# Edge loop of a graph-attention layer: two blocks per preparation step, eight row buffers instead of six, first gathers in steps

## What is computed

```python
h = (x @ W).reshape(n, H, C)
a_src = (h * att_src[None]).sum(-1)
a_dst = (h * att_dst[None]).sum(-1)
alpha = a_src[src] + a_dst[dst] + a_edge
alpha = jax.nn.leaky_relu(alpha, NEG_SLOPE)
amax = jax.lax.stop_gradient(jax.ops.segment_max(alpha, dst, num_segments=n))
ex = jnp.exp(alpha - amax[dst])
denom = jax.ops.segment_sum(ex, dst, num_segments=n)
att = ex / (denom[dst] + 1e-16)
msg = h[src] * att[:, :, None]
out = jax.ops.segment_sum(msg, dst, num_segments=n).reshape(n, H * C) + bias
```

## Time and profile before

| what | value |
|---|---|
| median of 3 runs | 3088.73 us (3086.78 to 3095.65) |
| profiled execution, its time | 3089.7 us |
| profiled execution, its span | 3087.9 us |
| the edge loop in it, first gather to last new maximum | 953.97 to 1392.77 us |
| PE, DVE, ACT, POOL busy over the whole span | 81%, 53%, 28%, 19% |
| mean granted TensorE clock | 0.883 |

### The profile page before, as it was taken

The page is one execution under the profiler, slowest core; times in us unless marked ns, Lnnn a source line. Parts: engine busy times, 40 slices in busy tenths (PEclk is TensorE's granted clock), DMA queues, the critical chain, the costliest instruction groups (busy, mean ns, idle before and its releaser), DMA issues. The chain is left out here.

```text
span 3087.9 us, 30949 instructions
## 1 busy us (share of the span) xinstructions
PE 2505.5 (81%) x10585; PEld 1594.7 (52%) x10585; DVE 1646.0 (53%) x3714; ACT 861.9 (28%) x1943; POOL 601.0 (19%) x567
## 2 busy tenths in 40 slices
PE   4877965999955888784578999999998769759886
PEld 1344545999943776672443455444554334534442
DVE  9999344222323888887235897708962432430000
ACT  2165110111112666662111465105631100101110
POOL 0000056355303444431110000000001001012221
PEclk9899966999976888887598999999999889779888
DMA  4000444766734555540533553215434031469996
GB/s 128 0 1 1 139 125 134 255 212 215 248 76 114 141 141 141 146 104 19 192 118 144 188 191 108 76 59 178 162 96 144 0 121 39 175 207 350 342 338 205
DMA packets 198728, 445.53 MB, mean 144 GB/s; under 512 B 26570, under 2 KB 48058, under 8 KB 198094
## 3 DMA queue, kind: packets, MB, share of 16 engines
q1 hardware_dynamic: 156942, 344.67, 33.5%
q0 software_dynamic: 41632, 98.89, 12.3%
HBM read 396.77 MB, written 49.05 MB: 144 GB/s over the span
## 5 line engine op out<-in xcount | busy, mean ns | idle before, releaser
L2166 PE MATMUL psum<-x_res,HH 125*128 125x512 f32 (+1 forms) x960 | 353.4, 527 | 18.2 <-DVE x_res L2356 18.2
L2166 PEld LDWEIGHTS psum<-x_res,HH 125*128 125x128 f32 x960 | 182.0, 193 | 178.9 <-issue 158.1
L1146 POOL DMA_INDIRECT recd<-edge_records,edge_slots x160 | 192.2, 1201 | 328.9 <-issue 322.5
L1506 POOL DMA_INDIRECT hg<-HT,srcidx x196 | 191.5, 977 | 300.8 <-PE psum L1626 172.2
L1667 ACT ACTIVATE hg<-hg,ex 128x129 f32<-128x129 f32 x784 | 235.2, 388 | 1.6
L1626 PE MATMUL psum<-hg,Dh 128*125 128x258 f32 x784 | 231.9, 460 | 4.3 <-DVE ACC L1569 2.9
L2156 PE MATMUL psum<-W,XO 128*125 128x512 f32 x480 | 211.9, 603 | 0.0
L1626 PEld LDWEIGHTS psum<-hg,Dh 128*125 128x125 f32 x784 | 177.1, 232 | 45.1 <-issue 6.2
L2932 PE MATMUL psum<-wd,XN 128*40 128x512 f32 (+1 forms) x704 | 167.7, 635 | 14.6 <-DMA wd<-in_L_ffn_W_down 14.6
L1180 PE MATMUL psum<-xgT,w 128*128 128x192 f32 x1024 | 175.3, 330 | 2.9 <-DMA w<-in_L_ffn_w 2.9
L1180 PEld LDWEIGHTS psum<-xgT,w 128*128 128x128 f32 x1024 | 168.7, 192 | 7.1 <-DMA w<-in_L_ffn_w 4.1
(11 more groups left out here) (508 smaller groups left out, 3942.3 us busy)
## 6 DMA issues: line engine op xcount, KB each, us to landing
wd<-in_L_ffn_W_down SPq DMA_DIRECT2D x30, 2560.0 KB
w<-in_L_ffn_w SPq DMA_DIRECT2D x64, 1024.0 KB, 12.2
MK<-CT SPq DMA_DIRECT2D x80, 625.0 KB
wu<-in_L_ffn_W_up SPq DMA_DIRECT2D x8, 2730.0 KB, 17.7
rows<-ROWS POOLq DMA_DIRECT2D x24, 625.0 KB, 7.5
w<-in_L_ffn_W SPq DMA_DIRECT2D x18, 512.0 KB
t<-in_L_ffn_tv_W SPq DMA_DIRECT2D x16, 512.0 KB
targets<-DROW SPq DMA_DIRECT2D x49, 128.0 KB
```

The source lines that it names most:

```text
L1146: pool.indirect_dma_start(out=g.recd, out_offset=bass.IndirectOffsetOnAxis(ap=g.posi[:, c:c + 1], axis=0), in_=g.E8[:, c, :], in_offset=No ...
L1506: pool.indirect_dma_start(out=hg[j % RING][:, c, :], out_offset=None, in_=g.HT, in_offset=bass.IndirectOffsetOnAxis(ap=g.srcidx[:, j * CH ...
L2166: return pe.matmul(flat[:, at:at + x1 - x0], HH[:, k, h * DH + c * 128:h * DH + c * 128 + 128], z[n % 4][:, x0:x1], start=(k == 0 and i < ...
```

## The change

It rewrites `gnn1_blocks`:

- Blocks go in pairs p = (2p, 2p+1), NP = 25. Slot terms, turn, rows and one-hots are made once per pair at double width. Slot terms of pair p+1 run in the even iteration j = 2p, its one-hots in the odd iteration j = 2p+1. Spread, largest, look-up, alpha, weights, sum and add stay per block.
- `Dh` and `q` have two buffers (of pairs) instead of three (of blocks). SP's loads are 25 of twice the size.
- `hg` is one tensor with eight row buffers. One semaphore counts the gathers of a pair, and the slot terms of a pair wait for all eight of them (L1526 in the changed file).
- Gathers of blocks 0 and 1 are issued at once. Those of blocks 2 to 7 wait for `rows` of pair j // 2 - 1 (`pool.wait_ge(*rows.at(j // 2))`): 2 and 3 for the slot terms of pair 0, and so on. From block 8 on block j waits until block j - 8 is summed.

```diff
-    HW, N4, RING = NH * (DH + 1), CH * NH, 6
+    HW, N4, RING, NP = NH * (DH + 1), 2 * CH * NH, 8, (NB + 1) // 2
...
     def pool_program():
         for j in range(NB):
             if j >= RING:
                 pool.wait_ge(*summed.at(j - RING + 1))
+            elif j >= 2:
+                pool.wait_ge(*rows.at(j // 2))
             for c in range(CH):
...
-    def dve_slot_terms(j):
-        u = j % 3
-        dve.wait_ge(*gathered[j % RING].at(64 * (j // RING + 1)))
-        step(dve.tensor_tensor(q[u][:], hg[j % RING][:, :, HW:HW + NH], rec(j)[:, :, 2:6], ALU.add))
-        if j:
-            dve.wait_ge(*turned.at(j))
+    def dve_slot_terms(p):
+        n, first = chunks(p), 2 * p % RING
+        dve.wait_ge(*gathered[p % (RING // 2)].at(128 * (p // (RING // 2)) + 16 * n))
+        found = hg[:, first:first + n // CH, :, HW:HW + NH].rearrange("p r c h -> p (r c) h")
+        step(dve.tensor_tensor(q[p % 2][:, 0:n, :], found, rec(p)[:, :, 2:6], ALU.add))
+        if p:
+            dve.wait_ge(*turned.at(p))
...
         dve_slot_terms(0)
         dve_onehots(0)
-        dve_slot_terms(1)
         tiles = {}
         for j in range(NB):
             tiles[j] = tile_of(dve, j)
             dve_largest(j)
             dve_new_max(j, tiles[j])
-            if j + 2 < NB:
-                dve_slot_terms(j + 2)
+            if j % 2 == 0 and j // 2 + 1 < NP:
+                dve_slot_terms(j // 2 + 1)
             if j >= 2:
                 dve_add_sums(j - 2, tiles[j - 2])
             dve_alpha(j)
-            if j + 1 < NB:
-                dve_onehots(j + 1)
+            if j % 2 == 1 and j // 2 + 1 < NP:
+                dve_onehots(j // 2 + 1)
...
             pe_look_up(j)
             if j + 1 < NB:
                 pe_spread(j + 1)
-            if j + 2 < NB:
-                pe_turn(j + 2)
+            if j % 2 == 0 and j // 2 + 1 < NP:
+                pe_turn(j // 2 + 1)
             if j:
                 pe_sum(j - 1)
...
             act_rescale(j)
-            if j + 2 < NB:
-                act_rows(j + 2)
+            if j % 2 == 0 and j // 2 + 1 < NP:
+                act_rows(j // 2 + 1)
             act_weights(j)
```

More of the change, by code:

```diff
@@ L1473, in gnn1_blocks @@
     v, selected = s.sig("dve_steps"), s.sig("selector_made")
-    gathered = [s.sig(f"gathered{u}") for u in range(RING)]
+    gathered = [s.sig(f"gathered{u}") for u in range(RING // 2)]
     loaded = [s.sig(f"counts_loaded{u}") for u in range(3)]
@@ L1484, in bank, with chunks, rec, half @@
         return g.PS[0:TP, k, :]
-    def rec(j):
-        return g.rec[:, j * CH:(j + 1) * CH, :]
+    def chunks(p):
+        return min(2, NB - 2 * p) * CH
+    def rec(p):
+        return g.rec[:, 2 * p * CH:2 * p * CH + chunks(p), :]
+    def half(j):
+        return j // 2 % 2, j % 2 * CH
     def tile_of(eng, j):
@@ L1495, in sp_program @@
     def sp_program():
-        for j in range(NB):
-            if j >= 3:
-                sp.wait_ge(*onehot.at(3 * (j - 2)))
-            sp.dma_start(drow[j % 3][:], bcast(g.DROW[j * BLK:(j + 1) * BLK], 128)).then_inc(*loaded[j % 3].up(16))
+        for p in range(NP):
+            if p >= 3:
+                sp.wait_ge(*onehot.at(3 * (p - 2)))
+            n = chunks(p) * 128
+            sp.dma_start(drow[p % 3][:, 0:n], bcast(g.DROW[2 * p * BLK:2 * p * BLK + n], 128)
+                         ).then_inc(*loaded[p % 3].up(16))
     def pool_program():
@@ new lines, in dve_slot_terms @@
+    def dve_slot_terms(p):
[5 more added lines that the diff above has]
+            dve.wait_ge(*turned.at(p))
+        split(dve, step, q[p % 2][:, 0:n, :].rearrange("p c h -> p (c h)"),
+              [q_parts[:, k, 0:n * NH] for k in range(3)], q_rest[:, 0:n * NH]).then_inc(*rows.up())
@@ L1600, in pe_spread @@
     def pe_spread(j):
-        pe.wait_ge(*rowsT.at(j + 1))
+        b, c0 = half(j)
+        pe.wait_ge(*rowsT.at(j // 2 + 1))
         if j:
@@ L1610, in pe_look_up @@
     def pe_look_up(j):
-        b = tile_of(pe, j)
+        tile, (b, c0) = tile_of(pe, j), half(j)
         pe.wait_ge(*newmax.at(j + 1))
@@ L1644, in pe_program, with act_rows @@
         pe_sum(NB - 1)
-    def act_rows(j):
-        act.wait_ge(*turned.at(j + 1))
-        if j >= 2:
-            act.wait_ge(*spread.at(j - 1))
-        act.activation(qT[j % 2][:], g.PS[0:3 * N4, 4, 0:128], ACT.Copy).then_inc(*rowsT.up())
+    def act_rows(p):
+        act.wait_ge(*turned.at(p + 1))
+        if p >= 2:
+            act.wait_ge(*spread.at(2 * (p - 1)))
+        act.activation(qT[p % 2][:], g.PS[0:3 * N4, 4, 0:128], ACT.Copy).then_inc(*rowsT.up())
     def act_rescale(j):
```

71 lines of the change are left out of this document (36 added, 35 removed).

## The result

The changed kernel took 3086.32 us (median; 3081.11 to 3089.94), beside 3091.4 us (3085.17 to 3096.29) for the kernel before on the same chip. The ratio is 0.9984, with an interval from 0.9976 to 0.9992: faster by 0.16%, 5.1 us. The profiled execution has a span of 3083.1 us, 4.8 less than before, at nearly the same granted clock (0.884, before 0.883).

What follows compares the result with a forecast made beforehand. While gathers run, matmul signals held behind POOL's bursts were taken to bound the loop, 8.38 us per block against 8.57 measured. Mid-loop 0, tail -3 and start +3 summed to 0: 3089 us, range 3068 to 3107.

Steps and rivals of the forecast that it cites:

- What bounds the loop: Mid-loop: signals held behind POOL's gathers make a two-block chain, 8.38 us per block; DVE's own chain is 7.72.
- The forecast drawn from it there: From the no-contention rule: gathers have no part in the late signals, DVE's time sets the pace, about 3071 us.
- Price of both edits while gathers run: 0. The cover is the held signal: Mid-loop: cheaper slot terms and one-hots save DVE 0.6 us per block, but the held signal hides it: 0.
- mid-loop 0: The middle of the loop while gathers run: the change was to gain or lose nothing there, 0 us.
- The rival of rarer breaks: Mid-loop: masks only in odd iterations break the hold less often, up to +8 us, 3097; chance 0.10.
- DVE's time counts: Mid-loop: 20 blocks without waits gain 0.6 us each, -12; with tail -3 and start -4, 3071 us; chance 0.32.
- Buffers. ... at the same place of the iteration: Mid-loop gathers still follow a sum, four at a time; eight buffers help only the loop's end, tail -3 us.
- With the cover gone: Mid-loop: were the held signal gone, DVE's shorter work would save 41 x 0.6 = 25 us.
- The start, +3: First gathers: -4 us from earlier data, +6 for three bursts of eight, +1 for loads; ends -4 and +19.
- the rival of held bursts: Start: bursts of eight hold every signal, costing +19 in place of +3, 3106 us; chance 0.18.
- The tail, -3: Loop's end: the last two blocks are fetched two blocks sooner, so more blocks run free of held signals, -3 us.
- Waits after: Profile after: DVE's idle time ahead of the masked maximum grows from 28 to about 50 us, nearly all "remote".

Runs made afterwards that it cites:

- e4: The kernel before with eight buffers and block j's gathers held until spread j - 3, nothing per pair: 3058.07 us, 0.9921 of the kernel before.
- e2: The kernel before with eight buffers and the first gathers waiting for rows, nothing per pair: 3089.77 us, 1.0031 of the kernel before.
- e16: The change with gathers of 4 numbers a row in place of 520, fourth run, kernel before at 3080.8 us: 1.0027 of the kernel before.
- e1: The change with six buffers in place of eight and the first 24 gathers at once: 3094.88 us, 1.0043 of the kernel before.
- e9: The kernel before, unchanged, run again for a trace in another session: 3053.36 us.
- e10: The change, unaltered, run again in the session of e9: 3053.59 us, 1.0014 of the kernel before.
- e3: The change with block j's gathers also held until spread j - 3: 3067.14 us, 0.9957 of the kernel before.
- e15: The change with all gathers behind the spread and one-hot DT made in the even iteration, second run: 3038.43 us, 0.9957 of the kernel before.

## Why the prediction was wrong

The forecast was 3089, no change. The time came within 3 us of that, but only since the gain in the middle and the loss in the start, both misjudged, nearly cancel; it was faster by 0.16%. Step by step:

*What bounds the loop* was right for the trace at hand. With no burst across a spread (e4) every "remote" wait of the middle is gone, and the pace is 7.95 where e2 has 8.30. DVE's chain was put at 7.72 and is that with 0.2 on it. What the prediction could not see from one trace is that the hold comes and goes with the session. The Trainium skill's rule (page "SBUF — State Buffer", section "Who interferes with whom") that a DMA never contends with a compute engine agrees with e16's pace, which is the same at 18 GB/s and at 146. The forecast drawn from it there, that the gathers have no part, fell with e2 and e4.

*"Price of both edits while gathers run: 0. The cover is the held signal"* is the step that failed, and with it "mid-loop 0". The saving itself was right: 0.6 us a block was said, DVE worked 0.61 less. But the held signal did not cover it. The wait ahead of the masked maximum was to take it all and grow from 28 to about 50 us; it is 30.7, and in the middle it grew by 4.2 where DVE saved 24.0. The wait for the sum took 8.4 more, and 15.2 were left as gain. The masked maximum behind the one-hots is no longer late: DVE comes to it later, and by then the signal is there, though POOL's burst runs on. The rival of rarer breaks had named the thing that may be behind this, with the wrong sign: it held that with a mask in every second iteration the breaks would go. It took the long gather for the mask's doing; in the earlier trace rows and in ten more bursts of the middle before, it is a gather begun inside Dh. In the change 19 of 39 blocks have such a gather, 1.20 to 1.91 us long. That the long gather is what lets the signal through fits the rows but was not tested. The rival "DVE's time counts" was closest in the middle: it gave -12, with a period near 8.0 and "remote" waits no longer than before. Its start of -4 was wrong.

*"Buffers. ... at the same place of the iteration", priced at nothing mid-loop*, may have failed as well. Without the eight buffers the pairs lose (e1, 14.2 us), for a reason that is shown: eight gathers must have landed before the slot terms. Whether eight buffers alone bring anything in the middle stays open, as said at e2.

*With the cover gone* the step promised 0.6 us a block. DVE then worked 0.66 less, but the pace fell by 0.18 only (e9 to e10), and it rose by 0.16 with the gathers behind the spread (e4 to e3). What took it back in e10 are the waits for the sum (15.7 us in the middle, 3.0 in e9) and 11.5 us ahead of the masked maximum, all of these in the iterations without one-hots. The prediction summed DVE's two iterations and did not ask whether PE's sum, which costs the same in both, fits the shorter one. With the one-hots spread over both (e15) the pace is 7.59, 0.36 below e9's, across sessions of one level.

*The start, +3*, was mis-sized: +8.7. The second and fourth new maxima came at 987.9 and 1005.6, for 989.4 and 1006.1 in the prediction. The prediction then priced each of the three groups that follow `rows` as a burst of eight. The last of them did not end there: the buffers of blocks 0 and 1 had been summed meanwhile, so POOL ran on through sixteen. By its own mark (the fourth after 1020) the rival of held bursts was not met, but its mechanism made the loss, one block later.

*The tail, -3*: the last gather comes 44.7 us ahead of the last new maximum, 29.6 before, so 15 earlier as said; it was worth 0.1.

*Waits after*: foreseen were about 50 us, nearly all with no engine named; there were 30.7, of which 20.2 are put down to the spread itself. They end where they were to end, about 1.05 us after the last gather of a burst (1.0 to 1.3), and in the iteration that was named. The period was to stay at 8.4 to 8.7 and was 8.16.

The sum of the parts is then +8.7 - 15.2 - 0.1, or -6.7 before rounding, where it had been +3 + 0 - 3.

## What to carry to other kernels

A trace shows one session, and the same program can run otherwise in the next: where a wait has no named cause and lasts as long as another engine's burst, run the kernel before again before pricing a change against that wait, and compare only within one session. A gain of 0.16% in one session, and a loss of 0.14% in another, is no gain to build on. Where the hold is there, take the burst off the path; with eight buffers and the gathers issued behind the spread the kernel before took 0.9921 of its time. When a wait is said to cover a saving, say how much longer it must then get, and look for that. And when work is made for two blocks at once, spread its pieces over both, and give the second block's data the buffers that it needs.

## What the runs showed of the hardware

- In three of seven sessions signals of TensorE's matmuls reached DVE and ACT late while GpSimd issued indirect gathers one behind another: up to 3.7 us behind four gathers, and 15.9 us (look-up ended 1007.24, alpha 1023.10) behind sixteen. In the burst of sixteen a sum of TensorE took 11 us itself, in place of 3.7 to 5.4. In the other four sessions no trace of any version has a wait of this kind in the loop; the change, traced in one of them, had the signal at once in the same burst. The program did not decide it, nor did the chip by itself: on one chip the kernel before took 3080.7 and 3051.8 us. With rows of 16 bytes (18 GB/s) the hold was still there, 13.0 us behind sixteen gathers. What differs between the sessions is open.
- A gather that begins inside a one-hot of DVE (tensor_scalar or tensor_tensor) ends about 0.82 us after that instruction's end and not 0.95 after its own start: 1.91 us behind the start of Dh, a tensor_tensor of 128x1000 that takes 1.19. The Trainium skill, page "SBUF — State Buffer", section "Who interferes with whom", has a DVE instruction with two SBUF inputs contend with a GpSimd instruction that reads SBUF. By that rule the trace agrees for Dh.
